# Doing 14 of 16 columns of the row-maximum chain between the two last reduces, in an attention and FFN kernel on eight cores

## The chip, the cores and the metric

The kernel runs on one Trainium2 chip, as the same program on all 8 of its cores, each with its own sequence of 2048 rows. There is no traffic between cores. The metric is the device time in microseconds of the slowest core. Each core has TensorE (PE in the profile; its weight loads are PEld), VectorE (DVE), ScalarE (ACT), GpSimd (POOL) and SyncE (SP), which run their own instruction streams and meet at semaphores.

## The reference

One layer over x of shape (8, 2048, 1024): an attention with a sink key, a layer norm, a linear layer with a low-rank addition, and a second layer norm.

```
q = x @ w_q.T + b_q            # 129 wide
k = x @ w_k.T + b_k            # 129 wide
v = x @ w_v.T + b_v            # 1024 wide
scores = q @ concat(k_0, k).T  # 2048 x 2049
attn = softmax(scores)
x = layernorm(x + (x + attn @ concat(v_0, v)))
W' = W + up_aux @ (lora_up @ (lora_down @ down_aux))
x = layernorm(x + (x @ W'.T + b))
```

## The kernel before

The sequence is cut into 16 tiles of 128 rows (NT = 16). All orders are written by hand; every engine has one list of instructions, and two semaphores count finished work: `t` is raised by TensorE, `v` by VectorE. A constant such as `T_PACKT` or `V_PACK` is the count at which a certain piece is finished, so `ve.wait_ge(t, T_PACKT)` holds VectorE until TensorE has raised `t` that often. `te.drain(...).then_inc(t, 1)` raises the count when TensorE has finished everything before it; `ve.drain()` lets VectorE finish what it has begun before the next instruction, which is needed where that instruction reads the result.

The stages run one behind the other:

1. Projections to QmT, KmT (128 x 2048) and the extra row in Qe2, Ke2; then V, tile by tile, into Vh.
2. Sink scores: 16 columns, one for each tile, copied to `ssink`.
3. Row maxima, the stage of the change. For each of 16 tiles of queries TensorE computes 128 x 2048 scores (L401 and L403, four pieces of 512 columns). Even tiles go to the accumulator `pq`, odd ones to the pair `pv[0]`, `pv[1]` of 1024 columns each. VectorE reduces an even tile by one instruction over 2048 columns into a column of `mcols` (L584), and an odd tile by two over 1024 columns into two columns of `modd` (L587 and L588). TensorE may write tile j when tile j - 2 is reduced.
4. The closing chain on VectorE (L591 to L601), over all 16 columns at once: the larger of the two halves of the odd tiles, the larger of that and the sink score, the negation to `negmb`, the sum with the sink score to `psd`, and the cast to `packf`. Each step reads what the one before wrote, so a drain stands between them. The last drain raises `v` to `V_PACK`.
5. On `V_PACK` TensorE transposes `packf` (L408), VectorE copies the result to `packTf` (L603), SyncE copies it into a row of `Qe2` (L313), and ScalarE computes an exponential of `psd` (L695) for the sink.
6. Scores a second time, transposed and with the negated maximum as an extra row (L418 and L422 don't need it and go ahead of it; L434 does), and ScalarE's exponentials (L700 on), two tiles in turn. TensorE's first matmuls on Ke, Qe here are the first that need stage 5's copy.
7. Attention times V (L455 to L457), first layer norm on VectorE (L610 to L639), forming of the weight W' (L471 to L485, called the weight stage below), the FFN (L512), second layer norm (L545 to L559) and the output.

The last tile of the FFN is already split in two signals: a drain stands between its halves (L520).

Of the kernel before, what the change touches and what calls it, by code (L numbers as in the profile page):

```python
# [9 lines left out]
AX = mybir.AxisListType.X  # L10
OP = mybir.AluOpType
# [4 lines left out]
NT = 16  # L16
# [9 lines left out]
T_VP0 = 3  # L26
T_PSK = 20
T_SA0 = 20
T_PACKT = 37
V_ONES = 1  # L30
V_VHONES = 2
V_VE0 = 2
# [4 lines left out]
SC_QM, SC_KM, SC_E2, SC_PSINK = 1, 2, 3, 4  # L37
T0B, SC0B = T_PACKT, SC_PSINK
TB = lambda tt: T0B + tt + 1
# [120 lines left out]
def build_nc(debug=False):  # L160
# [30 lines left out]
    with es:  # L191
# [9 lines left out]
        ssink = sb("ssink", [128, NT], F32)  # L201
        mcols = sb("mcols", [128, NT], F32)
        negmb = sb("negmb", [128, NT], BF16)
        psd = sb("psd", [128, NT], F32)
        packf = sb("packf", [128, 32], F32)
# [15 lines left out]
        modd = sb("modd", [128, NT], F32)  # L221
# [5 lines left out]
        t = es.enter_context(nc.semaphore("t"))  # L227
        v = es.enter_context(nc.semaphore("v"))
# [22 lines left out]
        pv = [pv0, pv1]  # L251
# [17 lines left out]
        with nc.Block() as blk:  # L269
# [66 lines left out]
            def _(te):  # L336
# [51 lines left out]
                for j in range(NT):  # L388
                    if j == 0:
                        te.wait_ge(v, V_SSINK)  # L390
                    elif j == 1:
                        te.wait_ge(v, V_VE0 + NT)
                    else:
                        te.wait_ge(v, V_M0 + (j - 2) + 1)
                    for n in range(NC4):
                        n0, n1 = n * 512, (n + 1) * 512
                        if j % 2 == 0:
                            outp = pq[:, n0:n1]
                        else:
                            outp = (pv[n // 2])[:, (n % 2) * 512:(n % 2 + 1) * 512]  # L400
                        te.matmul(outp, QmT[:, j * 128:(j + 1) * 128],  # L401
                                  KmT[:, n0:n1], start=True, stop=False)
                        te.matmul(outp, Qe2[:, j * 128:(j + 1) * 128],  # L403
                                  Ke2[:, n0:n1], start=False, stop=True)
                    te.drain(fusable=True).then_inc(t, 1)  # L405
                te.wait_ge(v, V_PACK)
                te.wait_ge(dsy, DSY_PRO)
# [156 lines left out]
            def _(ve):  # L564
# [14 lines left out]
                ve.wait_ge(t, T_PSK)  # L579
                ve.tensor_copy(ssink[:, :], pq[:, 0:NT]).then_inc(v, 1)  # L580
                for j in range(NT):
                    ve.wait_ge(t, T_SA0 + j + 1)
                    if j % 2 == 0:
                        ve.reduce_max(mcols[:, j:j + 1], pq[:, :], axis=AX).then_inc(v, 1)  # L584
                    else:
                        jo = j // 2
                        ve.reduce_max(modd[:, 2 * jo:2 * jo + 1], pv[0][:, :], axis=AX)  # L587
                        ve.reduce_max(modd[:, 2 * jo + 1:2 * jo + 2], pv[1][:, :],  # L588
                                      axis=AX).then_inc(v, 1)
                ve.drain()  # L590
                ve.tensor_tensor(bass.AP(mcols, 1, [[NT, 128], [2, 8]]),  # L591
                                 bass.AP(modd, 0, [[NT, 128], [2, 8]]),
                                 bass.AP(modd, 1, [[NT, 128], [2, 8]]), OP.max)
                ve.drain()
                ve.tensor_tensor(mcols[:, :], mcols[:, :], ssink[:, :], OP.max)
                ve.drain()
                ve.tensor_scalar_mul(negmb[:, :], mcols[:, :], -1.0)
                ve.drain()
                ve.tensor_tensor(psd[:, :], ssink[:, :], negmb[:, :], OP.add)
                ve.tensor_copy(packf[:, 0:16], negmb[:, :])  # L600
                ve.drain().then_inc(v, 1)  # L601
                ve.wait_ge(t, T_PACKT)
                ve.tensor_copy(packTf[0:16, :], pv[0][0:16, 0:128]).then_inc(v, 1)  # L603
# [45 lines left out]
                def v_va(_):  # L649
                    ve.memset(Bb, 0.0)  # L650
                    ve.wait_ge(t, T_A)
                    ve.tensor_copy(Ab, FO[0][0:4, :])
                    ve.drain().then_inc(v, 1)

                def v_vb(_):
                    ve.wait_ge(t, T_B)
                    ve.tensor_copy(Bb[0:50, :], FO[0][0:50, :])
                    ve.drain().then_inc(v, 1)
# [165 lines left out]
```

## Time and profile before

| | us |
|---|---|
| timed runs, median of 2 | 453.77 (453.25 to 454.3) |
| profiled execution, its own time | 453.97 |
| span of its slowest core (core 7) | 452.4 |
| span of the seven others | 442.6 to 445.6 |
| PE / DVE / ACT busy on core 7 | 372.4 / 227.2 / 105.6 |

The profile's time axis starts at the first instruction of a core, so the same piece of work stands at slightly other times on other cores. The row-maximum stage on core 7 goes from 121.8 to 159.5 us. Busy time of PE is that of pipelined matmuls, which overlap in the record: a matmul of 512 columns is shown with 0.38 us, but starts 0.22 us after the one ahead of it. Likewise two VectorE instructions with no drain between them overlap a little.

### The profile page before, as it was taken

The numbers are of one execution on the slowest core, as the hardware profiler recorded it, in microseconds if no ns is written. First come the engines' busy times: TensorE is split into PE (matmuls) and PEld (weight loads), VectorE is DVE, ScalarE is ACT, GpSimd is POOL, SyncE is SP. The second block draws the span as 40 slices with busy tenths as digits, with TensorE's granted clock in tenths as the row PEclk, the third lists the DMA queues.
The fourth block names the chain that finished last, engine by engine and source line by source line (L and its number), as shares of the span: only waits on it lengthen the run. The fifth ranks groups of instructions, "written<-read, shape, count | busy, mean of one in ns | idle before, by whom it ended". The sixth has DMA issues, their size and how long they took to land.

```text
span 452.4 us, 5173 instructions; the slowest of 8 cores (442.6 to 452.4 us)
## 1 busy us (share of the span) xinstructions
PE 372.4 (82%) x1861; PEld 157.1 (35%) x1861; DVE 227.2 (50%) x370; ACT 105.6 (23%) x119; POOL 22.9 (5%) x46
## 2 busy tenths in 40 slices
PE   1656899999888678889999999999847788999992
PEld 0211333333433223334444444444313343333330
DVE  7000033333399900004766677666688535676774
ACT  0202200000000048852121211212142232434232
POOL 8500000000000000010000000000120000000000
PEclk9996999999899969999999999999955559999998
DMA  8999300000000020024112113121291001232323
GB/s 123 167 162 170 62 0 0 1 0 1 0 1 1 0 93 0 1 36 124 51 48 74 68 48 95 46 89 51 52 159 24 0 1 46 95 138 96 139 95 138
DMA packets 11097, 28.25 MB, mean 62 GB/s; under 512 B 1856, under 2 KB 3008, under 8 KB 11072
## 3 DMA queue, kind: packets, MB, share of 16 engines
q0 software_dynamic: 5712, 10.52, 15.0%
q1 hardware_dynamic: 5360, 17.41, 10.9%
q8 instruction: 15, 0.25, 0.2%
q14 instruction: 10, 0.08, 0.1%
HBM read 29.50 MB, written 8.39 MB: 84 GB/s over the span
## 4 chain that ended last, share of the span: by engine, by line
issue 26%; DVE 24%; PEld 14%; PEldq 9%; DVEq 9%; DMA 8%; ACT 7%; POOL 3%; ACTq 0%; SPq 0%; POOLq 0%
DMA Ke<-PTsink 8%; PEld pv L375 5%; DVE pq L610 4%; DVE mcols L584 4%; PEld pq L512 4%; ACT o1s L720 4%; DVE X1f L639 3%; DVE st L628 2%; DVE ys L623 2%; PEldq L521 2%; DVEq L627 2%; DVE modd L587 2%; DVEq L630 2%; PEldq L437 2%; DVE modd L588 1%
## 5 line engine op out<-in xcount | busy, mean ns | idle before, releaser
L457 PE MATMUL pq<-Vh,AR 128*128 128x512 bf16 x256 | 97.2, 380 | 0.0
L456 PE MATMUL pq<-Vh,AR 128*128 128x512 bf16 x256 | 96.4, 377 | 0.0
L512 PE MATMUL pq<-Vh,AR 128*128 128x512 bf16 x256 | 62.3, 387 | 5.6 <-issue 4.5
L577 DVE TENSOR_TENSOR Vh<-pv,X1f 128x1024 bf16<-128x1024 f32 x16 | 19.6, 1226 | 84.7 <-PEq L379 84.7
L375 PE MATMUL pv<-AR 128*128 128x512 bf16 x256 | 57.8, 379 | 4.6 <-issue 3.5
L455 PE MATMUL pv<-Vh,AR 128*128 128x1 bf16 x256 | 42.0, 164 | 6.5 <-issue 4.8
L610 DVE SCALAR_TENSOR_TENSOR pq<-Vs,packf,pq 128x1024 f32<-128x1024 bf16 x16 | 20.6, 1288 | 48.5 <-PEq L458 45.9
L455 PEld LDWEIGHTS pv<-Vh,AR 128*128 128x128 bf16 x256 | 25.0, 98 | 42.7 <-issue 13.9
L512 PEld LDWEIGHTS pq<-Vh,AR 128*128 128x128 bf16 x256 | 24.3, 99 | 40.3 <-issue 15.1
L375 PEld LDWEIGHTS pv<-AR 128*128 128x128 bf16 x256 | 23.9, 97 | 38.5 <-issue 12.0
L456 PEld LDWEIGHTS pq<-Vh,AR 128*128 128x128 bf16 x256 | 24.5, 96 | 29.0
L720 ACT ACTIVATE o1s<-pq,smalls 128x1024 f32<-128x1024 f32 x16 | 17.8, 1115 | 59.3 <-DVEq L617 59.3
L343 PE MATMUL pq<-AR 128*128 128x512 bf16 x32 | 10.9, 467 | 21.3 <-DMA AR<-xT 21.3
L695 ACT ACT_TABLE_LOAD x1 | 1.3, 1283 | 105.8 <-DVEq L601 105.8
L457 PEld LDWEIGHTS pq<-Vh,AR 128*128 128x128 bf16 x256 | 24.5, 96 | 0.0
L623 DVE SCALAR_TENSOR_TENSOR ys<-xs,o1s 128x512 f32<-128x512 f32 x16 | 11.1, 691 | 21.1 <-ACT o1s L720 21.1
L748 ACT ACTIVATE o1s<-xs,smalls 128x1024 f32<-128x1024 f32 x15 | 18.6, 1241 | 11.3 <-DVEq L561 11.3
L729 ACT ACTIVATE AR<-ptb 128x1024 bf16<-128x1024 bf16 x16 | 16.2, 1020 | 20.9 <-PEq L499 20.9
L584 DVE TENSOR_REDUCE mcols<-pq 128x1 f32<-128x2048 f32 x8 | 18.2, 2281 | 3.6 <-PEq L405 3.6
L545 DVE TENSOR_TENSOR xs<-X1f,pq 128x512 f32<-128x512 f32 x15 | 10.3, 688 | 16.2 <-PEq L521 16.2
L725 ACT ACTIVATE smalls<-mvp,smalls 128x1 f32<-128x1 f32 x16 | 4.7, 294 | 48.8 <-DVEq L632 48.8
L401 PE MATMUL pq<-KmT,QmT 128*128 128x512 bf16 x32 | 13.1, 408 | 2.8 <-DVE mcols L584 2.3
(127 smaller groups left out, 446.4 us busy)
## 6 DMA issues: line engine op xcount, KB each, us to landing
xs<-x SPq DMA_DIRECT2D x16, 512.0 KB, 3.2
out<-o1s SPq DMA_DIRECT2D x15, 512.0 KB, 2.6
AR<-xT POOLq DMA_DIRECT2D x7, 512.0 KB, 20.0
AR<-wvT POOLq DMA_DIRECT2D x8, 256.0 KB, 31.0
Vh<-WT POOLq DMA_DIRECT2D x8, 256.0 KB, 6.6
AR<-wqkT POOLq DMA_DIRECT2D x8, 64.5 KB, 15.7
X1f<-bvb SPq DMA_DIRECT2D x1, 512.0 KB, 3.3
AR<-xT POOLq DMA_DIRECT2D x2, 256.0 KB, 7.2
```

Source lines behind the costliest of these rows:

```text
L375: ins = te.matmul(pv[tt % 2][:, n0:n1], XT[:, c * S + tt * 128: c * S + (tt + 1) * 128], wvb[:, c * D + n0: c * D + n1], start=(c == 0), s ...
L455: te.matmul(PL[j % 2][:, 0:1], lhs, r3_, start=first, stop=last)
L456: te.matmul(PO[j % 2][:, 0:512], lhs, r1_, start=first, stop=last)
L457: te.matmul(PO[j % 2][:, 512:1024], lhs, r2_, start=first, stop=last)
L512: te.matmul(FO[j % 2][:, n0:n1], X1T[:, c * S + j * 128: c * S + (j + 1) * 128], WeffT[:, c * D + n0: c * D + n1], start=(c == 0), stop=False)
L577: ve.tensor_tensor(Vh[:, tt * VW: tt * VW + D], pv[tt % 2][:, :], bvbs[:, :], OP.add).then_inc(v, 1)
L584: ve.reduce_max(mcols[:, j:j + 1], pq[:, :], axis=AX).then_inc(v, 1)
L610: ve.scalar_tensor_tensor(PO[p][:, :], Vs[:, 0:D], packf[:, 16 + j:17 + j], PO[p][:, :], OP.mult, OP.add)
L623: ve.scalar_tensor_tensor(ys[p][:, 0:512], xs[p][:, 0:512], 2.0, o1s[p][:, 0:512], OP.mult, OP.add)
L720: s.activation(o1s[p][:, :], PO[p][:, :], AF.Identity, scale=rls[p]).then_inc(sc, 1)
L729: s.activation(bass.AP(PT, j * 128, [[NT * S, 128], [S, ND], [1, 128]]), ptb[j % 2][:, :], AF.Copy).then_inc(sc, 1)
L748: s.activation(o1s[p][:, :], xs[p][:, :], AF.Identity, bias=nmrp[p], scale=r1p[p]).then_inc(sc, 1)
```

## The change

In the last odd tile (15), VectorE no longer runs its two reduces back to back. After the first it works through the chain of stage 4 for the first 14 columns, whose tiles are all reduced by then, and only then reduces the second half; after that the chain is run for the two columns that are left, 14 and 15. So that the first half can be reduced before the second is written, TensorE signals it by a drain of its own (`T_SA15H`), and the counts behind it go up by one.

```
+T_SA15H = 36
+T_SAF = lambda j: T_SA0 + j + 1 if j < NT - 1 else 37
-T_PACKT = 37
+T_PACKT = 38
...
                         te.matmul(outp, Qe2[:, j * 128:(j + 1) * 128],
                                   Ke2[:, n0:n1], start=False, stop=True)
+                        if j == NT - 1 and n == 1:
+                            te.drain(fusable=True).then_inc(t, 1)
                     te.drain(fusable=True).then_inc(t, 1)
...
                 for j in range(NT):
-                    ve.wait_ge(t, T_SA0 + j + 1)
                     if j % 2 == 0:
+                        ve.wait_ge(t, T_SAF(j))
                         ve.reduce_max(mcols[:, j:j + 1], pq[:, :], axis=AX).then_inc(v, 1)
-                    else:
+                    elif j < NT - 1:
+                        ve.wait_ge(t, T_SAF(j))
                         jo = j // 2
                         ve.reduce_max(modd[:, 2 * jo:2 * jo + 1], pv[0][:, :], axis=AX)
                         ve.reduce_max(modd[:, 2 * jo + 1:2 * jo + 2], pv[1][:, :],
                                       axis=AX).then_inc(v, 1)
+                    else:
+                        ve.wait_ge(t, T_SA15H)
+                        ve.reduce_max(modd[:, 14:15], pv[0][:, :], axis=AX)
+                        ve.drain()
+                        ve.tensor_tensor(bass.AP(mcols, 1, [[NT, 128], [2, 7]]),
+                                         bass.AP(modd, 0, [[NT, 128], [2, 7]]),
+                                         bass.AP(modd, 1, [[NT, 128], [2, 7]]),
+                                         OP.max)
+                        ve.drain()
+                        ve.tensor_tensor(mcols[:, 0:14], mcols[:, 0:14],
+                                         ssink[:, 0:14], OP.max)
+                        ve.drain()
+                        ve.tensor_scalar_mul(negmb[:, 0:14], mcols[:, 0:14], -1.0)
+                        ve.drain()
+                        ve.tensor_tensor(psd[:, 0:14], ssink[:, 0:14],
+                                         negmb[:, 0:14], OP.add)
+                        ve.tensor_copy(packf[:, 0:14], negmb[:, 0:14])
+                        ve.wait_ge(t, T_SAF(j))
+                        ve.reduce_max(modd[:, 15:16], pv[1][:, :],
+                                      axis=AX).then_inc(v, 1)
                 ve.drain()
```

Behind it the five operations of the chain stay, with their drains, on columns 14:16 instead of all 16 (the first of them on column 15 alone).

VectorE's instructions from the reduce of tile 14 to the cast of packTf were these before (the drains aren't listed; a name before the arrow is what is written, `[waits t]` is a wait for TensorE's count):

```order
33 L584 TENSOR_REDUCE mcols<-pq 128x1 [waits t]
34 L587 TENSOR_REDUCE modd<-pv 128x1 [waits t]
35 L588 TENSOR_REDUCE modd<-pv 128x1
36 L591 TENSOR_TENSOR mcols<-modd 128x8
37 L595 TENSOR_TENSOR mcols<-mcols,ssink 128x16
38 L597 TENSOR_SCALAR negmb<-mcols 128x16
39 L599 TENSOR_TENSOR psd<-ssink,negmb 128x16
40 L600 CAST packf<-negmb 128x16
41 L603 CAST packTf<-pv 16x128 [waits t]
```

And now the same stretch from the first reduce of tile 15 on:

```order
34 L597 TENSOR_REDUCE modd<-pv 128x1 [waits t]
35 L599 TENSOR_TENSOR mcols<-modd 128x7
36 L604 TENSOR_TENSOR mcols<-mcols,ssink 128x14
37 L607 TENSOR_SCALAR negmb<-mcols 128x14
38 L609 TENSOR_TENSOR psd<-ssink,negmb 128x14
39 L611 CAST packf<-negmb 128x14
40 L613 TENSOR_REDUCE modd<-pv 128x1 [waits t]
41 L616 TENSOR_TENSOR mcols<-modd 128x1
42 L619 TENSOR_TENSOR mcols<-mcols,ssink 128x2
43 L622 TENSOR_SCALAR negmb<-mcols 128x2
44 L624 TENSOR_TENSOR psd<-ssink,negmb 128x2
45 L626 CAST packf<-negmb 128x2
```

The second reduce has moved behind five small operations, and has a wait of its own; the list is five instructions longer, 360 instead of 355.

TensorE's instructions at the end of the stage stand as before, here with the new line numbers: the last matmul of tile 15, the transpose that waits for VectorE, the matmuls that run ahead and those that need the copy. Only the added drain, which isn't listed, is new.

```order
220 L405 MATMUL pv<-Ke,Qe 128x512
221 L412 MATMUL pv<-idf,packf 16x128 [waits v,dsy]
222 L422 MATMUL pq<-QmT,KmT 128x512 [waits v]
223 L422 MATMUL pq<-QmT,KmT 128x512 x3
224 L426 MATMUL pv<-QmT,KmT 128x512 [waits v]
225 L426 MATMUL pv<-QmT,KmT 128x512 x3
226 L438 MATMUL pq<-Qe,Ke 128x512 [waits dlp]
```

What is queued behind the transpose is all of stages 6 and 7.

## Rows read from the trace of the kernel before

**Rows 1.** The view of the cores: span and mean granted TensorE clock of each.
```profile
core 1: 445.6 us, clock 0.952
...
core 7: 452.4 us, clock 0.928
```

**Rows 2.** The totals of the waits, core 7: total us, times, longest.
```profile
DVE mcols L584 <- PEq L405: 3.6, 1, 3.6
```

**Rows 3.** Timeline of VectorE, core 7, tiles 14 and 15: start, duration, instruction.
```profile
153.77 2.28 DVE L584 TENSOR_REDUCE mcols<-pq 128x1 f32<-128x2048 f32 x1
156.01 1.23 DVE L587 TENSOR_REDUCE modd<-pv 128x1 f32<-128x1024 f32 x1
157.16 1.21 DVE L588 TENSOR_REDUCE modd<-pv 128x1 f32<-128x1024 f32 x1
158.46 0.17 DVE L591 TENSOR_TENSOR mcols<-modd 128x8 f32<-128x8 f32 x1
158.70 0.17 DVE L595 TENSOR_TENSOR mcols<-mcols,ssink 128x16 f32<-128x16 f32 x1
158.96 0.17 DVE L597 TENSOR_SCALAR negmb<-mcols 128x16 bf16<-128x16 f32 x1
159.20 0.17 DVE L599 TENSOR_TENSOR psd<-ssink,negmb 128x16 f32<-128x16 f32 x1
159.29 0.17 DVE L600 CAST packf<-negmb 128x16 f32<-128x16 bf16 x1
160.24 0.28 DVE L603 CAST packTf<-pv 16x128 bf16<-16x128 f32 x1 [0.78 <-PEq L410]
```

**Rows 4.** Timeline of TensorE, core 7; in brackets the idle time before and its end.
```profile
155.08 0.38 PE L403 MATMUL pv<-Ke,Qe 128*128 128x512 bf16 x1
...
155.51 0.38 PE L403 MATMUL pv<-Ke,Qe 128*128 128x512 bf16 x1
159.74 0.37 PE L408 MATMUL pv<-idf,packf 128*16 128x128 f32 x1 [3.85 <-DVEq L601]
...
163.71 1.91 PE L434 MATMUL pq<-Qe,Ke 128*128 128x512 bf16 x4
```

**Rows 5.** Window 122 to 158 us, core 7: busy by PE, PEld, DVE, ACT, POOL; PEclk; DMA.
```profile
122.00:158.00 36.00, 28.21 (x120) 10.54 (x119) 35.63 (x24) 0.00 (x0) 0.00 (x0) 1.00 0.00 1
```

**Rows 6.** Timeline of TensorE, core 7, last two FFN tiles, from half to half.
```profile
436.81 0.38 PE L516 MATMUL pq<-KmT,Qe 128*128 128x512 bf16 x1
437.03 1.89 PE L512 MATMUL pq<-Vh,AR 128*128 128x512 bf16 x8
...
441.20 0.38 PE L516 MATMUL pq<-KmT,Qe 128*128 128x512 bf16 x1
441.66 1.90 PE L512 MATMUL pq<-Vh,AR 128*128 128x512 bf16 x8
```

**Rows 7.** Groups of instructions by form, core 7: busy, mean ns, idle before.
```profile
L613 DVE TENSOR_TENSOR pv<-pv,packf 128x1 f32<-128x1 f32 x16 | 2.5, 159 | 0.0
```

**Rows 8.** Timeline of ScalarE, core 7: the first exponential of stage 6.
```profile
165.74 1.88 ACT L700 ACTIVATE AR<-pq 128x2048 bf16<-128x2048 f32 x1 [4.66 <-PEq L437]
```

**Rows 9.** Timelines of TensorE and ScalarE on core 2.
```profile
159.22 0.27 PE L408 MATMUL pv<-idf,packf 128*16 128x128 f32 x1 [3.86 <-DVEq L601]
...
164.15 1.88 ACT L700 ACTIVATE AR<-pq 128x2048 bf16<-128x2048 f32 x1 [3.60 <-PEq L437]
```

**Rows 10.** Window 352 to 374 us, columns as in rows 5: core 7, then core 5.
```profile
352.00:374.00 22.00, 17.93 (x77) 7.89 (x76) 9.16 (x11) 7.17 (x7) 0.00 (x0) 0.50 0.00 1
...
352.00:374.00 22.00, 16.91 (x117) 8.29 (x116) 12.83 (x19) 9.25 (x10) 0.00 (x0) 0.99 0.00 1
```

**Rows 11.** Timeline of VectorE, the statistics of FFN tile 14: core 5, then core 7.
```profile
432.73 0.69 DVE L551 BATCH_NORM_STATS2 st<-xs 128x6 f32<-128x512 f32 x1
...
440.62 0.69 DVE L551 BATCH_NORM_STATS2 st<-xs 128x6 f32<-128x512 f32 x1
```

More of the change, by code:

```diff
@@ L590, in _ @@
                 ve.drain()
-                ve.tensor_tensor(bass.AP(mcols, 1, [[NT, 128], [2, 8]]),
-                                 bass.AP(modd, 0, [[NT, 128], [2, 8]]),
-                                 bass.AP(modd, 1, [[NT, 128], [2, 8]]), OP.max)
+                ve.tensor_tensor(mcols[:, 15:16], modd[:, 14:15], modd[:, 15:16],
+                                 OP.max)
                 ve.drain()
-                ve.tensor_tensor(mcols[:, :], mcols[:, :], ssink[:, :], OP.max)
+                ve.tensor_tensor(mcols[:, 14:16], mcols[:, 14:16],
+                                 ssink[:, 14:16], OP.max)
@@ L596, in _ @@
                 ve.drain()
-                ve.tensor_scalar_mul(negmb[:, :], mcols[:, :], -1.0)
+                ve.tensor_scalar_mul(negmb[:, 14:16], mcols[:, 14:16], -1.0)
                 ve.drain()
-                ve.tensor_tensor(psd[:, :], ssink[:, :], negmb[:, :], OP.add)
-                ve.tensor_copy(packf[:, 0:16], negmb[:, :])
+                ve.tensor_tensor(psd[:, 14:16], ssink[:, 14:16],
+                                 negmb[:, 14:16], OP.add)
+                ve.tensor_copy(packf[:, 14:16], negmb[:, 14:16])
```

## Prediction

> **What bounds the kernel now.** I read the spans of the cores first [rows 1]: core 7 is the slowest at 452.4 us, and the next slowest, core 1, needs 445.6 us. The profiled execution took 453.97 us, so 1.57 us lie around core 7's span, and it stands 0.2 us above the 453.77 us median of the timed runs. Sums are made on core 7 and put on 453.77.
>
> The change sits in the row-maximum stage, where VectorE reduces 16 tiles of scores that TensorE writes. The totals of the waits [rows 2] say who is late there: in front of its 2048-wide reduces VectorE waited for TensorE once, 3.6 us before the first tile, and then never again, so the stage goes at VectorE's pace. TensorE waited 3.85 us at its transpose (L408) for VectorE's closing drain (L601) [rows 4]. So what VectorE does from the last reduce to that drain is bare, and the timeline of VectorE shows it without a hole [rows 3]: tile 14 starts at 153.77, tile 15 at 156.01 and 157.16, the first small operation at 158.46, the cast to packf at 159.29. TensorE's timeline [rows 4] has the last matmul of tile 15 at 155.51, ending at 155.89, which is before VectorE even begins the tile at 156.01. Then TensorE is idle until 159.74.
>
> That is the observation on which everything rests: **the second half of tile 15 lies ready 1.27 us before VectorE could read it** (157.16 less 155.89). There is no wait in front of the second reduce under which work could be put. TensorE's granted clock was 1.00 (2.4 GHz) from 122 to 158 us [rows 5], so tile 15 isn't late by a slow clock either.
>
> **The change part by part.**
>
> *The early signal on TensorE.* One more drain between the halves of tile 15. The kernel has the same split in its last FFN tile: there the step from the last matmul of the first half to the next is 0.46 us (441.20 to 441.66), against 0.22 us in the tile ahead, which has no drain (436.81 to 437.03) [rows 6]. So it costs TensorE 0.24 us: tile 15 ends at about 156.13. The first half is complete at 155.46 at the latest (the matmul of 155.08 is already in the second half) [rows 4], and VectorE comes for it at 156.01, for the second half not before 157.16. Cost on the path 0; the cover is 0.5 us for the first half and 1 us or more for the second, and if it were gone the cost would be the 0.24 us.
>
> *The first reduce of tile 15 no longer overlaps the second.* Without a drain between them the starts are 1.15 us apart (156.01 to 157.16). With a drain behind it the second reduce took 1.30 us to the next start (157.16 to 158.46) [rows 3]. Cost 0.15 us.
>
> *Five operations put in between the two reduces* (the maximum over 7 odd tiles, the maximum with the sink, the negation, the sum, the cast, over 7 or 14 columns). Their twins of 8 or 16 columns stand in the trace: start to start 0.24 (158.46 to 158.70), 0.26, 0.24 and 0.09 us [rows 3], sum 0.83. From the cast to the second reduce there is no drain: at least the 0.09 us of the undrained step above, at most the cast's own 0.17. Columns don't matter at this size: 8 columns took 0.17 us, 16 took 0.17, and a 128x1 operation took a mean of 159 ns [rows 7]. Together 0.92 to 1.00 us, bare, since VectorE is the late engine. The new waits (for the first half, then for the full tile) are both met before VectorE gets to them; the drainless step between two reduces is as long with a wait as without (tile 14 to 15 with one: 153.77 to 156.01 is 2.24 us for a 2.28 us operation) [rows 3], so 0.
>
> *The tail behind the second reduce keeps its five operations*, each now on 1 or 2 columns. What shrinks is at most the 0.17 us of a row to the 0.16 of a 128x1 operation, 0.01 us each, 5 times: a gain of 0.05 us at most [rows 3, 7]. The drains between them stay.
>
> Sum: 0.15 + (0.92 to 1.00) - (0 to 0.05) = 1.02 to 1.15 us later at the drain that releases TensorE and ScalarE; I take **1.1 us**. What isn't in the trace is a small operation in front of a reduce, and a chain on 1 or 2 columns. I bound them by 0.6 (the 0.15 and five steps at the undrained 0.09) and 1.45 (the 0.15 and five steps at 0.26), and stay near the middle, since four of the five steps are the very pairs that the trace has.
>
> *Who is behind it.* On VectorE nothing but the cast L603, which waits for TensorE anyway. On TensorE the transpose L408 and everything after it; on ScalarE the exponential for packf, and on SP, behind the copy into Qe2, the first loads of x; the results of both are used only in the attention products, a stage later, so neither is late. The path runs through L408, L603, the copy, and the matmuls L434 to ScalarE's first exponential at 165.74 [rows 8]. All of it hangs on the drain, and from there TensorE is the bound, so a delay is carried to the end: nothing in the later stages is timed from anything but this chain.
>
> One rule of the Trainium skill speaks on the price. The page VectorE: DVE Perf Modes, section Rules for kernel authors, advises for chained operations to minimize their count, not the semaphores, and its section on the DRAIN holds that a wait between operations costs nothing extra. The first half speaks against this change as the trace does. [...]
>
> **The rivals.**
>
> *TensorE comes back to a slow clock for longer (slower).* TensorE's idle stretch grows from 3.85 to about 4.7 us, and its matmuls behind it start at 1.2 GHz already. On core 2 the clock rose in time for the matmuls L434, and from the transpose to the first exponential it took 4.93 us (159.22 to 164.15) [rows 9]; on core 7 L434 still ran slowly (four in 1.91 us) and it took 6.00 us (159.74 to 165.74) [rows 4, 8]. So a core that is now like core 2 may lose 1.07 us more; core 7 has paid it already, and may lose less if its clock rises at the same moment as before: two of those four would then run at the fast step of 0.22 us [rows 6] instead of 0.43, which takes 0.4 us off the 1.1. It decides if the slowest core is one of the first kind: 453.77 + 1.1 + 1.07 = 456.0 us.
>
> *The low clock in the weight stage falls on no core, or on a worse place.* Core 7 stands apart from its neighbours by one stretch. From 352 to 374 us core 5 was granted 0.99 and ran 117 matmuls, core 7 was granted 0.50 (1.2 GHz) and ran 77 [rows 10]; the missing 40, at the fast step of 0.22 us, are 8.8 us. Near the end core 5 starts the same operation at 432.73 and core 7 at 440.62 [rows 11]: a price of 7.9 us. Both run the same program, so it isn't the kernel that chose core 7. If no core draws it, the end is that of core 1: 454.9 - 6.8 = 448.1 us. For it: 7 of 8 cores escaped. Against it: all three executions I have lie between 453.25 and 454.3, so in each some core was held. If a core is held twice as long, the price is paid again: 462.8 us. The Trainium skill, page TensorE: Matmul & The Clock Gate, Part 1, says that the place of the rise varies from run to run of one kernel; the spread over the cores here agrees (core 2 and core 7 in [rows 4, 9]).
>
> *The inserted work is hidden after all (faster).* If the second half of tile 15 arrived after the block was done, the block would be free and the first reduce too: 1.15 us gained, 452.6 us. It needs the half at 156.01 + 1.15 + 1.1 = 158.3 or later; it is there at 155.9 to 156.1. TensorE would have to be 2.2 us later, at a clock that isn't granted low in this stage on core 7 [rows 5].
>
> **How the numbers follow.** Forecast: 453.77 + 1.1 = 454.9 us, chance 0.62 (its own range, with both bounds of the cost, the 0.4 us that core 7 may hide and the half microsecond between runs: 453.6 to 456.0). Longer slow clock behind the gap, 456.0: 0.14. No core held, 448.1: 0.12. Held twice, 462.8: 0.05. Hidden, 452.6: 0.03. The rest, 0.04, I give to what I haven't seen. The first two together hold 0.76, so a range of eight in ten has to reach to the case in which no core is held: 447.6 to 457.0. Two per cent, about what a measurement of this kernel can tell from no change, is 9.1 us; only the double hold comes near. Faster by more 0.02, within 0.95, slower by more 0.03.
>
> **What would show it.** In the profile of the changed kernel VectorE's timeline should have the two reduces of tile 15 some 2.2 us apart instead of 1.15, with five small operations between them, no idle time before the second, and the same chain of five behind it at the same steps. TensorE's wait at the transpose should grow from 3.85 to about 4.8 us, and from the start of tile 15's first reduce to the cast of packTf it should be about 5.3 us, not 4.2. In the FFN and attention stages nothing should differ but the start. I am wrong if VectorE shows a wait before the second reduce, if the tail's steps shrink below 0.2 us, or if the time moves by more than 2 us on a core whose clock is as before.

## The result, and the profile after

The changed kernel takes 456.97 us in the median (455.39 to 458.67, 20 runs), the kernel before 453.25 us (446.94 to 455.36, 19 runs): 3.7 us more, 0.8%. The ratio of the runs that are compared is 1.0138, 95% interval 1.0105 to 1.017, which is slower, and within the 2% that count as the same. It is larger than the ratio of the medians because for the kernel before the comparison keeps its quicker runs only. Forecast were 454.9 us, so the direction and the order of VectorE's work were right and the size was not: 1.1 us stood in the sum, 3.7 were measured.

The view of the cores of the changed kernel; before, one core of eight was above 446 us [rows 1].

```profile
core 3: 446.7 us, clock 0.941
core 4: 451.3 us, clock 0.932
core 5: 456.2 us, clock 0.922
core 6: 453.5 us, clock 0.928
```

The four others stand at 454.2, 454.1, 453.5 and 451.7 us (cores 0, 1, 2 and 7). Only core 3 is near where seven cores were before. The slowest is core 5, and its VectorE timeline answers to [rows 3]:

```profile
156.40 2.28 DVE L588 TENSOR_REDUCE mcols<-pq 128x1 f32<-128x2048 f32 x1
158.60 1.21 DVE L597 TENSOR_REDUCE modd<-pv 128x1 f32<-128x1024 f32 x1
159.89 0.17 DVE L599 TENSOR_TENSOR mcols<-modd 128x7 f32<-128x7 f32 x1
160.13 0.17 DVE L604 TENSOR_TENSOR mcols<-mcols,ssink 128x14 f32<-128x14 f32 x1
160.38 0.18 DVE L607 TENSOR_SCALAR negmb<-mcols 128x14 bf16<-128x14 f32 x1
160.63 0.17 DVE L609 TENSOR_TENSOR psd<-ssink,negmb 128x14 f32<-128x14 f32 x1
160.72 0.17 DVE L611 CAST packf<-negmb 128x14 f32<-128x14 bf16 x1
160.80 1.22 DVE L613 TENSOR_REDUCE modd<-pv 128x1 f32<-128x1024 f32 x1
162.11 0.16 DVE L616 TENSOR_TENSOR mcols<-modd 128x1 f32<-128x1 f32 x1
...
162.91 0.16 DVE L626 CAST packf<-negmb 128x2 f32<-128x2 bf16 x1
163.85 0.28 DVE L629 CAST packTf<-pv 16x128 bf16<-16x128 f32 x1 [0.78 <-PEq L414]
```

The reader should see that there is no bracket with idle time before the second reduce (L613): nothing was waiting there. The reduces start 2.20 us apart instead of 1.15, so the block costs 1.05 us, and the tail is as long as it was (162.11 to 162.91 is 0.80 us, before 158.46 to 159.29 was 0.83). From the first reduce of tile 15 to the cast of packTf it is 5.25 us; before it was 4.23.

TensorE and ScalarE on the same core, answering to [rows 4, 8]:

```profile
157.27 0.38 PE L405 MATMUL pv<-Ke,Qe 128*128 128x512 bf16 x1
157.73 0.39 PE L403 MATMUL pv<-KmT,QmT 128*128 128x512 bf16 x1
...
163.35 0.37 PE L412 MATMUL pv<-idf,packf 128*16 128x128 f32 x1 [4.58 <-DVEq L627]
...
167.32 1.91 PE L438 MATMUL pq<-Qe,Ke 128*128 128x512 bf16 x4
```

```profile
169.35 1.88 ACT L726 ACTIVATE AR<-pq 128x2048 bf16<-128x2048 f32 x1 [4.66 <-PEq L441]
```

The early signal opens a step of 0.46 us (157.27 to 157.73), as forecast. The wait at the transpose has grown from 3.85 to 4.58 us, a little less than the 4.7 to 4.8 forecast, because TensorE's own last matmul is also later by the 0.24 us of the drain. The four matmuls L438 still take 1.91 us, at the slow rate, and from the transpose to the first exponential it is 6.00 us. Read on all cores, that stretch was 4.93 to 5.05 us on seven cores before and 6.00 on core 7; now it is 5.99 or 6.00 us on six, 5.65 on one and 4.64 on core 3. The low clock behind the gap lasts 6.8 us on seven cores; before, it lasted 3.4 us on seven and 6.8 on core 7 alone.

And in the weight stage, the window of [rows 10] a little longer (350 to 372 us); core 5 of the changed kernel, then core 7 of the kernel before:

```profile
350.00:372.00 22.00, 17.34 (x80) 7.61 (x79) 13.51 (x15) 6.46 (x7) 0.00 (x0) 0.50 0.00 1
```

```profile
350.00:372.00 22.00, 17.60 (x80) 8.01 (x79) 10.21 (x12) 7.17 (x7) 0.00 (x0) 0.50 0.00 1
```

They are alike: 80 matmuls at 0.50. Before, core 7 alone was at 0.50 through this window; in the profile after, it is all of them but core 3, which came back at 363.0 us. The granted clock read in steps of one microsecond gives these stretches at 1.2 GHz (start to end in us, length in brackets):

```
before, core 7:      329.6 to 373.9 (44.4)       the others: 23.9 or 27.3 long, over by 354.8
after,  core 5:      333.4 to 377.8 (44.4)       likewise cores 0, 1, 2 and 6
after,  core 3:      325.5 to 363.0 (37.5)
after,  core 4:      328.4 to 342.1, 345.5 to 372.8
after,  core 7:      328.4 to 338.6, 345.4 to 372.7
```

Every run lists its cores' spans, and these fall in two groups, below 450 us and above. I call a core **held** when its span is 450 us or more; the number is fixed, so an edit that shifts both groups shifts them against it (see e6 and e7). Before, over the 62 runs that are listed with their cores (496 spans), 99 cores were held, 0.20, and in 10 runs none was. After, it is 147 of 168, 0.88, and there is no run without one. The 19 runs of the kernel before that were timed together with the change have no list of cores, but five of them took less than 450 us, so in those no core was held either. The means of the two groups are 445.2 and 453.3 us before (the 24 runs beside e1) and 446.9 and 453.2 us after. These two pairs can't be compared to the microsecond: the 24 runs were slower than the 19 (455.02 against 453.25 us in the median).

### The profile page after: what moved, and what is told of

Same layout as the page of the kernel before. It is cut to its first block, busy times and chain, and to the rows that moved or that the text cites. A ratio compares the mean times of both kernels' runs of the same rounds, so it can differ in the third digit from the quotient of the medians.

```text
span 456.2 us, 5184 instructions; the slowest of 8 cores (446.7 to 456.2 us)
## 1 busy us (share of the span) xinstructions
PE 373.5 (82%) x1861; PEld 157.3 (34%) x1861; DVE 227.8 (50%) x375; ACT 105.7 (23%) x119; POOL 22.8 (5%) x46
## 4 chain that ended last, share of the span: by engine, by line
issue 27%; DVE 23%; PEld 14%; PEldq 9%; DVEq 9%; ACT 7%; DMA 7%; POOL 2%; ACTq 0%; SPq 0%; POOLq 0%
DMA AR<-xT 6%; PEld pv L377 5%; DVE pq L636 4%; PEld pq L516 4%; ACT o1s L746 4%; DVE mcols L588 3%; DVE X1f L665 3%; DVE st L654 2%; DVE ys L649 2%; PEldq L525 2%; DVEq L653 2%; DVEq L656 2%; PEldq L441 2%; DVE modd L592 2%; DVE modd L593 1%
## 5 line engine op out<-in xcount | busy, mean ns | idle before, releaser
L345 PE MATMUL pq<-AR 128*128 128x512 bf16 x32 | 9.5, 416 | 24.0 <-DMA AR<-xT 24.0
L549 DVE TENSOR_TENSOR xs<-X1f,pq 128x512 f32<-128x512 f32 x15 | 10.3, 687 | 16.3 <-PEq L525 16.3
L403 PE MATMUL pv<-KmT,QmT 128*128 128x512 bf16 x32 | 12.4, 389 | 3.8 <-DVE modd L593 3.5
```

## The experiments

**e1, the early signal alone.** VectorE as before, TensorE with the new drain.

```
+                        if j == NT - 1 and n == 1:
+                            te.drain(fusable=True).then_inc(t, 1)
...
-                    ve.wait_ge(t, T_SA0 + j + 1)
+                    ve.wait_ge(t, T_SAF(j))
```

> The kernel before with the extra drain between the halves of score tile 15 on TensorE, and nothing moved on VectorE. Theory A (the change costs its 1.05 us of bare VectorE work, and the rest of the 3.7 us comes from TensorE's clock, which falls differently because the chain is later): the drain moves nothing on the chain, so this is the time of before within 1 us, and most cores end near 445 us as before. Rival B (the split of the tile on TensorE is what disturbs the clock): 456 to 457 us and most cores above 451 us.

Measured: 454.9 us, before 455.02 (ratio 0.9939, 0.9891 to 0.9986); 16 of 80 cores held, 0.20. The signal costs nothing that these runs can tell.

**e2, e3, e4, a delay that has nothing to do with the change.** 4, 8 and 14 repeats of one step of the chain in the kernel before.

```
                 ve.tensor_tensor(mcols[:, :], mcols[:, :], ssink[:, :], OP.max)
                 ve.drain()
+                for _ in range(4):
+                    ve.tensor_tensor(mcols[:, :], mcols[:, :], ssink[:, :], OP.max)
+                    ve.drain()
```

> The kernel before, with the maximum with the sink score repeated four times more on VectorE (each repeat leaves the same values), so the closing drain comes 1.0 us later by work that has nothing to do with the change. Theory A: any delay of this size does what the change does: 456.5 to 457.5 us, TensorE's low clock at the transpose lasts 6.8 us instead of 3.4 on most cores and most cores end above 451 us. Rival B (it is something of the change itself, the split tile or the order of the reduces): 453.25 + 1.0 = 454.3 us, and most cores end near 446 us.

> The same with eight repeats, 2.0 us. Theory A: what counts is where the chain stands against the changes of the clock, not how much later it is. With 2.0 us the low clock at the transpose should last 6.8 us on nearly all cores, and the time should be 457 to 459 us. Rival C (the time simply grows with the delay, and the extra is the same for every delay): 457 + 1.0 = 458 us, so this run alone tells little; it is the middle point for the next.

> The same with fourteen repeats, 3.4 us, the difference between the two lengths (3.4 and 6.8 us) that the low clock at the transpose has on the cores of both profiles. Theory A: the chain stands to the clock's changes as in the kernel before, only 3.4 us later, so the weight stage should again be slow for 24 to 27 us on most cores and not for 44: most cores end at 445 + 3.4 = 448 to 449 us, and the median is 453.25 + 3.4 = 456.7 us, no more than e3 although the delay is 1.4 us longer. Rival C: 453.25 + 3.7 + 2.4 = 459.4 us, with most cores above 455 us.

Measured: e2 457.85 us (ratio 1.0073, 1.0026 to 1.0119), 33 of 72 cores held, 0.46. e3 458.69 us (1.0087, 1.006 to 1.0113), 32 of 40, 0.80. e4 459.82 us (1.0136, 1.0082 to 1.019), 55 of 80, 0.69. VectorE's timeline of e2, core 4, shows the four repeats in one row, and 1.00 us from their start to the next step:

```profile
161.64 0.93 DVE L598 TENSOR_TENSOR mcols<-mcols,ssink 128x16 f32<-128x16 f32 x4
162.64 0.17 DVE L600 TENSOR_SCALAR negmb<-mcols 128x16 bf16<-128x16 f32 x1
```

One microsecond of useless repetition costs 2.8 us over the 455.02 us beside it, so an excess over the work isn't of the change's own making. The next microsecond costs 0.8 us more (e3) and the 1.4 us after it 1.1 us (e4), about what they are long: the excess comes once. Two forecasts failed. In e2 fewer than half of the cores were held where I had most of them, although the low clock at the transpose lasted 6.8 us on six of the eight profiled. And my picture of e4 fell: with 3.4 us the chain should have stood to the clock as before, with few cores held, and 0.69 were. The times of e4 decide nothing between theory A and rival C: both were written from 453.25 us, and from the 455.02 us beside the run they would be 458.4 and 461.1 us, with 459.82 in the middle.

**e5, VectorE's move alone**, the counterpart of e1.

```
-                        if j == NT - 1 and n == 1:
-                            te.drain(fusable=True).then_inc(t, 1)
```

(against the changed kernel, with the counts set back)

> The changed kernel without TensorE's early signal: VectorE's order is that of the change, and both reduces of tile 15 wait for the whole tile. The counterpart of e1, and the same 1.05 us later on VectorE as e2. Theory A (a delay on VectorE is all that matters): as the changed kernel, 457 us, and at least seven cores in ten end above 450 us. Rival D (e2, with the same delay made otherwise, had 46 in 100 cores above 450 us against 83 for the change, so signal and move act together): like e2, about 457 us by the slowest core but only half of the cores above 450 us.

Measured: 459.15 us (four runs; ratio 1.0107, 1.0046 to 1.0168), 29 of 32 cores held, 0.91. The move alone does all that the change does (4.6 us over the 454.52 us beside it); e1 and e5 together leave nothing to the signal. Rival D, half of the cores, fell. Against e2 it has nearly the same delay and twice the share of held cores; e2's lower share has no explanation here.

**e6, TensorE kept at work in the gap before the transpose**, in the kernel before.

```
+                te.wait_ge(v, V_M0 + 15)
+                for i in range(14):
+                    te.matmul(pq[:, (i % 4) * 512:(i % 4 + 1) * 512], QmT[:, 0:128],
+                              KmT[:, 0:512], start=True, stop=True)
                 te.wait_ge(v, V_PACK)
```

> The kernel before, with 14 more matmuls on TensorE (512 columns each, into pq, which is free there and written anew afterwards) between score tile 15 and the transpose, so that TensorE works through the 3.85 us gap. Theory A (the low clock behind this gap is one cause and each core's place against the clock's changes another): the clock stays at 1.00 at the transpose, L418 to L434 run at the fast step, ScalarE's first exponential comes 1 to 2 us earlier, and the cores that aren't held in the weight stage end at 443 to 445 us; how many are held may change either way. Rival E (the low clock behind the gap decides by itself which cores are held later, since the core with 6.8 us there was the one held in both profiles of unchanged work): with no low clock there no core is held, and the time is 446 to 447 us.

Measured: 454.52 us, as before (454.52; ratio 1.007, 1.0025 to 1.0116), 57 of 80 cores held, 0.71. Every core gains 1 to 2 us at the gap here, and the upper group begins at 448 us: 68 of 80 spans are 448 us or more, 0.85, against 0.21 beside them. Core 6, window 155 to 165 us, the gap and the matmuls behind it; then 346 to 372 us:

```profile
155.00:165.00 10.00, 8.65 (x39) 3.38 (x37) 7.61 (x11) 1.50 (x2) 0.00 (x0) 1.00 0.00 0
...
346.00:372.00 26.00, 20.96 (x93) 9.37 (x94) 14.54 (x16) 8.26 (x9) 0.00 (x0) 0.50 0.00 1
```

The low clock behind the gap is gone on all eight cores (1.00), and the first exponential follows the transpose after 3.8 us (on core 5 160.92 to 164.68) instead of 4.9 to 6.0. Yet nearly four times as many cores are held as in the runs beside it (0.18). That refutes rival E: the low clock at the transpose doesn't choose the held cores. A chain that is early by 1 to 2 us is held as readily as one that is late by as much, and what was won at 160 us was lost at 350; seven of the eight profiled cores are at 1.2 GHz for 44.4 us, from 328 to 331 us on, and the eighth is there twice within that stretch.

**e7 and e8, the first wait of the weight stage filled**, before and changed. In this stage TensorE forms two small products, A and B, and then eight combinations, each of which adds the low-rank part to one piece of the weight (four matmuls of 512 columns), with the eight transposes of one tile of the sequence between every two of them.

```
+_TORDER = ([("tp", 0), ("tp", 1), ("A", 0), ("warm", 0), ("tp", 2), ("B", 0), ("tp", 3)]
...
+                def emit_warm(_):
+                    te.wait_ge(v, VC_RL(NT - 2))
+                    for i in range(26):
+                        te.matmul(pv0[:, 0:512], Vh[:, 8192:8320],
+                                  Vh[:, 8704:9216], start=True, stop=True)
```

> The kernel before, with 26 more matmuls (512 columns, into a part of pv0 that nothing reads, from parts of Vh that nothing writes) on TensorE in the weight stage, between the product A and the transposes of tile 2, where TensorE waits 6.2 us for ScalarE. Theory A (the price of a held core is paid because TensorE enters the weight stage from this gap at 1.2 GHz and stays there for 24 to 44 us): the clock stays at or near 1.00 from 326 us on, no core is held, all cores end within 3 us of each other, and the time is 440 to 446 us. Rival F (the weight stage loses its clock by itself, from its many short waits, whatever precedes it): the clock falls again some microseconds later, cores are held as often as before, and the time stays at 453 to 455 us.

> The changed kernel with the same 26 matmuls in the weight stage. Theory A (of the 3.7 us that the change costs, 1.05 are work on VectorE, up to 1.07 the longer low clock at the transpose, and the rest is that more cores are held in the weight stage): with the hold gone, it stands 1.0 to 2.2 us behind e7. Rival F: it stays at 457 us.

Measured: e7 454.78 us (ratio 1.0, 0.9971 to 1.0029), 53 of 80 held, and 68 of 80 at 448 us or more; e8 457.33 us (1.005, 1.0008 to 1.0092), 60 of 88 held. e7 was to take 440 to 446 us, and e8 to stand 1.0 to 2.2 us behind it; that distance is 2.55 us in the median and 1.0 in the mean over the cores. Filling the first wait didn't take the price away; it even raised the share, and the time stayed the same. But these two told where to look. Of e7's cores, core 5 ended at 443.1 us, core 7 at 453.0. Core 5 in two windows, then TensorE's timeline of core 5 and of core 7 at the third combination:

```profile
326.00:346.00 20.00, 13.44 (x80) 6.20 (x80) 16.10 (x28) 7.47 (x9) 4.52 (x8) 0.91 0.74 106
346.00:372.00 26.00, 19.91 (x139) 9.71 (x138) 17.67 (x24) 10.19 (x11) 0.00 (x0) 1.00 0.00 1
```

```profile
345.86 0.38 PE L484 MATMUL pq<-QmT,Vh 128*128 128x512 bf16 x1 [2.56 <-DVEq L671]
...
348.16 0.38 PE L484 MATMUL pq<-QmT,Vh 128*128 128x512 bf16 x1 [0.34 <-issue]
```

```profile
346.03 0.38 PE L484 MATMUL pq<-QmT,Vh 128*128 128x512 bf16 x1 [1.66 <-DVEq L671]
...
348.77 0.59 PE L484 MATMUL pq<-QmT,Vh 128*128 128x512 bf16 x1 [0.34 <-DVE Ke L654]
```

On both TensorE idles here for VectorE, which has the layer norm of tile 15 to do before it can take out the first combination. On core 7 the matmul of 346.03 is still quick and that of 348.77 slow (0.59): the clock fell just behind this wait. On six cores of e7 the last low stretch began between 344.6 and 346.9 us, the same moment at which it began the second time on the cores 4 and 7 of the changed kernel; it ended at 371.9 to 374.2 us on five of them and at 366.7 on core 3, which ended at 449.7 us.

**e9 to e12, that wait filled.** e9 in the kernel before: 24 matmuls before tile 2's transposes, 3 before product B, 2 before the first and 10 before the third combination; e10 the same in the changed kernel; e11 is e9 with e6; e12 has the ten before the third combination alone, and its edit is the one shown (`ct` is a combination, counted from 0).

```
+_WARM = {('ct', 2): 10}
+_TORDER = [y for x in _TORDER
+           for y in ([("warm", _WARM[x])] if x in _WARM else []) + [x]]
```

> The kernel before, with more matmuls on TensorE in all the longer waits of the weight stage: 24 before the transposes of tile 2, 3 before product B, 2 before the first and 10 before the third combination, where TensorE waits up to 2.9 us for VectorE. In e7, which filled only the first wait, the clock fell near 345 us on seven cores, after this wait, and stayed low to 372; core 5, where it didn't, ended at 443.1 us. Theory G (a core is held when the clock falls in or stays low through the wait near 345 us): no core is low from 346 to 372, share of cores above 450 us under 0.1, time 444 to 448 us. Rival F (the stage loses its clock whatever is filled): some cores low again by 350 us, the share 0.2 or more, 453 to 455 us.

> The changed kernel with the same matmuls as e9. Theory G: with no core held, only the 1.05 us of VectorE work and the longer low clock at the transpose (up to 1.07 us) are left of the change: 1.0 to 2.2 us above e9, where the plain kernels differ by 3.7 us in the median and by 5.6 us in the mean over the cores. Rival: it stays at 456 us or more, and the change has a cost that isn't this hold.

> e9 with the 14 matmuls of e6 before the transpose of the row maxima. e6 brought the first exponential 1.2 to 2.2 us closer to the transpose and had it taken back by held cores. Theory G: with no core held the gain shows: 1 to 2 us below e9, the fastest version, 443 to 446 us. Rival: as e9.

> The kernel before, with only the 10 matmuls before the third combination. Theory G: these ten are the ones that count where the clock has come back before 345 us, but without the first fill it is still low there on most cores, so the share of held cores falls only in part, from 0.2 to between 0.05 and 0.15, and the median stays at 452 to 455 us or falls to 448. Rival F: no difference from before.

Measured, beside 454.34 us for the kernel before (four runs each, ten of e12):

| | us | ratio, 95% interval | held |
|---|---|---|---|
| e9 | 444.01 | 0.983, 0.9709 to 0.9951 | 0 of 32 |
| e10 (changed) | 445.61 | 0.9875, 0.9779 to 0.9972 | 0 of 32 |
| e11 | 443.85 | 0.982, 0.9722 to 0.9918 | 0 of 32 |
| e12 | 448.59 | 0.9929, 0.9884 to 0.9974 | 0 of 80 |

Core 0 of e9 in two windows:

```profile
326.00:346.00 20.00, 15.62 (x87) 6.53 (x87) 15.97 (x27) 7.35 (x9) 2.77 (x6) 1.00 0.78 107
346.00:372.00 26.00, 19.62 (x138) 9.81 (x139) 17.61 (x25) 10.47 (x11) 0.00 (x0) 1.00 0.03 11
```

And core 0 of e12, before and behind the ten matmuls, with the row of the ten themselves:

```profile
329.00:345.00 16.00, 11.25 (x48) 4.99 (x49) 13.09 (x19) 7.21 (x8) 1.91 (x3) 0.50 0.62 93
350.00:372.00 22.00, 16.91 (x117) 8.35 (x116) 13.58 (x19) 8.20 (x10) 0.00 (x0) 1.00 0.00 1
```

```profile
342.54 4.42 PE L531 MATMUL pv<-Vh 128*128 128x512 bf16 x10 [0.23 <-issue]
346.75 0.59 PE L487 MATMUL pq<-QmT,Vh 128*128 128x512 bf16 x1
```

e12 changes least: the weight stage is entered at 0.50 as before, ten matmuls that compute nothing of use stand before the third combination, and of 80 cores none is held, where 22 of 104 were in the runs beside it. All eight cores of its profile rise at 347 to 349 us, where the ten matmuls end. The ten aren't hidden in the wait: in the kernel before it is 1.2 or 1.3 us long on every core, and at 1.2 GHz they take 4.4 us. So e12 also brings a delay at this place, and its cores end at 445.2 us in the mean, 1.2 us above the cores that weren't held beside it. The same delay without matmuls was not run, so that their work and not the delay keeps the clock up is argued. I had given it a share of 0.05 to 0.15; none was left. e9 also keeps the clock up in front of that, which is worth 4.6 us more in the median. e10 stands 1.6 us above e9 in the median and 1.7 us in the mean over the cores (442.8 against 441.1). e11 is the quickest version, but by 0.2 us in the median only, not the 1 to 2 expected; its cores' mean is 1.3 us below that of e9 (439.8 against 441.1), and its slowest cores stand apart from the rest.

## Why the prediction was wrong

*The wait that isn't there.* Right. The second half lay ready, and no idle time stands before the second reduce.

*The block, 1.02 to 1.15 us, taken as 1.1.* Right: 1.05. The steps were 0.24, 0.25, 0.25, 0.09 and 0.08 us, the extra drain behind the first reduce gave 1.29 instead of 1.15. (The forecast's own range is not quite what its terms give: 453.77 + 0.6 - 0.4 - 0.5 to 453.77 + 1.45 + 0.5 is 453.5 to 455.7 us, not 453.6 to 456.0. The 456.97 us lie outside either.)

*The tail keeps its length, the signal is free.* Right: 0.80 against 0.83 us, and e1.

*The rival of the longer slow clock behind the gap, up to 1.07 us, chance 0.14.* Its price was right and its chance too low: seven cores of eight had it in the profile after. With no core held (e9, e10) the change costs 1.6 us, which is the 1.05 and about half of the 1.07; in the profile of e10 the low clock behind the gap lasts 6.8 us on five cores of eight, in that of e9 on none. The forecast should have had this as its own term, since TensorE's work restarts a microsecond later on every core, and the sum would have been 1.6 and not 1.1.

*The hold in the weight stage.* Here the prediction failed. It read the price rightly (7.9 us; the two groups of spans are 8.1 apart before) and then wrote "Both run the same program, so it isn't the kernel that chose core 7", and left the share of held cores as it was: the term for it in the sum was nothing. It allowed for none being held or for a core held twice, and not for nearly all being held once. The program does set that share: 0.20 before and in e1, 0.46 to 0.91 with any delay on VectorE, 0.71 with the chain brought forward (e6), 0 with ten matmuls before the third combination (e12). The sentence ahead of it, "nothing in the later stages is timed from anything but this chain", fell with it: where the clock falls and rises times them too.

*Why the larger share costs the slowest core only some 2 us.* The time is that of the slowest of eight. Before, in 52 of 62 runs some core was held already, so the price had mostly been paid. What is new is that the core whose chain is late anyway is now held too. In the profile after, tile 15's first reduce starts between 153.86 us (core 3) and 158.60 (core 5), and core 5 is held and is the slowest; before, core 3 had the latest chain (157.53 us) and ended at 445.1 us, unheld. The seven held cores of the profile after end almost in the order of their chains: 451.3 and 451.7 us where that reduce starts before 154.8, 453.5 to 454.2 where it starts at 154.85 to 155.92, and 456.2 at 158.60. Of the 3.7 us then 1.6 are direct, by e10 less e9, two times four runs with the filled waits, and the other 2.1 are what is left for the larger share; that the late chains make them up was read from these profiles and not tested by itself.

*What stays open.* Why the kernel before is held so seldom, when a shift of its chain by 1 to 3.4 us either way is held more often. Where the chain stands when the clock changes has something to do with it, since every shift moved the share, but e4 came out against the simple form of that, and e2 and e5, whose delays are the same to 0.05 us, have shares of 0.46 and 0.91. Cores of e2 and e3 that stood alike at the start of the weight stage came out differently. Also open is how much of the share belongs to the chip: e1 to e4, e5 to e8 and e9 to e12 were timed on three chips, though the kernel before gave 0.18 to 0.21 on each. And the changed kernel was not run by itself beside e9 and e10, so the 3.7 and the 1.6 us come from runs that weren't timed together.

## What to carry to other kernels

Work moved ahead of the last operation of a stage hides only if that operation waits; look for the idle bracket in front of it before splitting a chain, since a split chain is paid twice. Where one core of several shows a long stretch at 1.2 GHz, ask what share of the cores shows it over many runs, not what it costs once: an edit of one microsecond elsewhere can multiply that share. And where a stage of short matmuls runs at 1.2 GHz, matmuls that nobody reads are worth a trial in the waits of TensorE there; here ten of them took 5.8 us off the median (0.7% by the ratio, interval 0.3 to 1.2), and 39 in four waits took off 10.3 us (1.7%, 0.5 to 2.9), more than the change was about. Filling one wait alone, and not that one, did nothing for the time (e7).

## What the runs showed of the hardware

The granted clock fell and rose at nearly the same places of the program on all cores, but not always: at the TensorE wait near 345 us it fell on six cores of e7, was low already on one and stayed up on core 5. The wait of core 5 was 2.56 us, longer than the 1.66 us of core 7, where it fell; on the five others where it fell the wait was 2.8 to 3.8 us. Once low there it stayed low through most of the next 26 us, in which TensorE was busy for 21 (20.96 on core 6 of e6), and rose at 371.9 us or later on five of the six. The same stage, entered at 0.50 (e12) or at 1.00 (e9), was granted full clock from 350 to 372 us on every profiled core when ten more matmuls stood before the third combination.

The trace agrees with the Trainium skill, page TensorE: Matmul & The Clock Gate, section Why this matters for your kernels, which warns of idle stretches between bursts of matmuls: the wait at the transpose (4.58 us on core 5 of the changed kernel) was followed by the low clock on every core, and in e6, with the wait filled, on none. Its Part 1 calls the cost of the clock's return under 1% of a typical kernel. Here a held core ended 8.1 us or 1.8% later than the others (453.3 against 445.2 us, the runs beside e1), so for the slowest core the measurement decides.
